# A five-stage transformer kernel: state sums as accumulating transposes, and two of eight input products on TensorE

## The reference

```
xc, z  = split(layernorm(x) @ W_in.T)              # 512 channels each
xc     = silu(causal_conv4(xc) + conv_b)
delta, Bm, Cm = split(xc @ W_x.T)                  # 64 + 16 + 16
delta  = softplus(delta @ W_dt.T + b_dt)
h[t]   = exp(delta[t] * A) * h[t-1] + delta[t] * Bm[t] * xc[t]   # 16 states a channel
y      = sum over the 16 states of h * Cm, plus Dp * xc
x     += (y * silu(z)) @ W_out.T
```

## Time and profile before

| | us |
|---|---|
| median of 3 runs | 2305.53 (2303.75 to 2313.75) |
| the profiled execution's own time | 2302.67 |
| its span | 2300.9 |
| TensorE busy, mean granted clock | 1823.9, 0.899 |
| VectorE busy | 1546.7 |
| ScalarE busy | 1047.7 |
| POOL busy | 1245.8 |
| scan L1074, 128 times | 292.6 |
| POOL's product L1009, 128 times | 301.7 |
| TensorE's sums L822, 512 passes | 246.9 |
| input products L1068, 128 times | 157.7 |

### The profile page before, as it was taken

One profiled execution on the slowest core, in us unless ns is written; L12 is line 12 of the kernel. 1 busy time (PEld: TensorE's weight loads), 2 busy tenths in 40 slices (PEclk: granted clock), 3 DMA queues, 4 the chain that ended last, 5 costly groups with the idle time before them and its releaser, 6 DMA issues. The chain is left out here.

```text
span 2300.9 us, 37782 instructions
## 1 busy us (share of the span) xinstructions
PE 1823.9 (79%) x10904; PEld 1250.3 (54%) x10905; DVE 1546.7 (67%) x3360; ACT 1047.7 (46%) x3013; POOL 1245.8 (54%) x999
## 2 busy tenths in 40 slices
PE   6799968988898668999869999798547999998000
PEld 6478833343433243677538888466414888877000
DVE  7699829999999968333447777577796333335633
ACT  1667637666666323333147777555225333332000
POOL 2688617777777710788415555365002555554775
PEclk9799989999999977999989999899666999999555
DMA  9121012312121052899601111000503999997332
GB/s 292 35 96 54 8 62 120 104 44 91 57 78 70 1 163 76 231 296 249 153 10 34 34 34 29 20 2 2 197 0 110 287 283 290 287 284 226 114 114 87
DMA packets 163772, 271.45 MB, mean 118 GB/s; under 512 B 28690, under 2 KB 97780, under 8 KB 162676
## 3 DMA queue, kind: packets, MB, share of 16 engines
q1 hardware_dynamic: 103028, 173.97, 23.4%
q0 software_dynamic: 30464, 68.19, 11.7%
q10 hardware_dynamic: 30144, 27.62, 3.5%
HBM read 218.17 MB, written 51.53 MB: 117 GB/s over the span
## 5 line engine op out<-in xcount | busy, mean ns | idle before, releaser
L1009 POOL TENSOR_TENSOR b_h<-b_h,b_bcb 128x1024 f32<-128x1024 f32 x128 | 301.7, 2359 | 115.4 <-DVE b_h L1074 115.0
L1583 POOL DMA_INDIRECT m1x_xb<-scratch_xn,m_tok x192 | 182.8, 952 | 316.2 <-issue 196.9
L1074 DVE TENSOR_TENSOR_SCAN b_h<-b_dA,b_pbx 128x1024 f32<-128x1024 f32 x128 | 292.6, 2286 | 4.4
L822 PE MATMUL b_psy<-b_h,ident 128*128 128x512 f32 x512 | 246.9, 611 | 56.0 <-POOL b_h L1009 56.0
L1630 PE MATMUL m1x_psh<-m1x_xe,m1x_w 128*128 128x128 f32 x1536 | 208.5, 279 | 11.2 <-issue 10.8
L1630 PEld LDWEIGHTS m1x_psh<-m1x_xe,m1x_w 128*128 128x128 f32 x1536 | 188.4, 193 | 19.2 <-issue 18.5
L822 PEld LDWEIGHTS b_psy<-b_h,ident 128*128 128x128 f32 x512 | 93.2, 192 | 191.7 <-POOL b_h L1009 104.6
L1772 DVE TENSOR_TENSOR m1x_hT<-m1x_sg,m1x_psh 128x128 f32<-128x128 f32 x192 | 55.3, 288 | 207.4 <-ACT m1x_sg L1718 138.3
L956 ACT ACTIVATE b_dA<-b_delta,b_A 128x504 f32<-128x504 f32 x256 | 166.1, 705 | 52.4 <-DVE b_h L1074 49.9
L1958 POOL TENSOR_TENSOR x_s<-x_s,x_rs 128x1024 f32<-128x1024 f32 x64 | 121.1, 1893 | 126.9 <-DVE x_rs L2124 126.9
L1068 DVE TENSOR_TENSOR b_pbx<-b_pdx,b_bcb 128x1024 f32<-128x1024 f32 x128 | 157.7, 1232 | 20.5 <-ACT b_pdx L939 13.8
(11 more groups left out here) (452 smaller groups left out, 4330.9 us busy)
## 6 DMA issues: line engine op xcount, KB each, us to landing
m1x_w<-in_m_w SPq DMA_DIRECT2D x192, 256.0 KB
b_bcb<-scratch_bc_rows SPq DMA_DIRECT2D x64, 512.0 KB, 4.7
scratch_y<-m1x_yb ACTq DMA_DIRECT2D x192, 128.0 KB
m_w<-in_m_w SPq DMA_DIRECT2D x64, 368.0 KB
a_c<-in_ctxT SPq DMA_DIRECT2D x16, 512.0 KB, 4.7
m_w<-in_m_w SPq DMA_DIRECT2D x64, 128.0 KB
x_area<-in_ctxT SPq DMA_DIRECT2D x32, 256.0 KB
m_w2all<-in_m_w SPq DMA_DIRECT2D x1, 8192.0 KB
```

Of the source, the lines that this page charges most:

```text
L822: mm = pe.matmul(psy[:, k % 2, :], ident[:, :], h[:, u % HB, j, :], start=False, stop=(nq == NQ - 1 and j == CQ - 1))
L1009: q.tensor_tensor(hs, hs, bcb[:, 1, CQ * nq:CQ * nq + CQ], ALU.mult).then_inc(sem("hc"), 1)
L1074: v.tensor_tensor_scan(h[:, u % HB].rearrange("p j n -> p (j n)"), dA[:, u % DB].rearrange("p j n -> p (j n)"), pbx[:, :, :].rearrange("p ...
L1583: g.indirect_dma_start(out=xb[:, j, :], out_offset=None, in_=xn, in_offset=bass.IndirectOffsetOnAxis(ap=tok[:, b:b + 1], axis=0)).then_inc ...
```

## The change

- `stage_mla`: the products of `turn` become accumulating transposes (`is_transpose=True`). On TensorE `output(t - 3)` is called before `queries(t + 1, 0)`, on ScalarE `exps(t - 1)` before `turned(t - 2, 0)`.
- `stage_mamba`, sums: `summed` turns h while it accumulates, 8 transposes of 128 x 128 in place of 2 products of 512 columns, so that `psy` holds tokens x channels. It has one buffer (one bank) now. The gate z is therefore computed by tokens: Z for 384 channels, the new piece W for the last 128. After the gate the new piece Y turns y back to channels (4 transposes and a copy), once a chunk.
- `stage_mamba`, inputs: for the pairs nq = 3 and 7 (TQ) the product dx * B is made on TensorE: dx is turned once a chunk (piece E), B of these pairs is computed by tokens once a group (piece U) and spread to diagonals (piece P, 16 copies of 128 columns on ScalarE), and `turned_inputs` multiplies the two, 8 products of 128 columns, two steps ahead. VectorE keeps six products of eight.
- Buffers: `pbx` two, `pdx` one, h five. B is broadcast for six pairs only.
- The last group's first three output parts stand together before its last `summed`; the last part is turned first.
- `stage_moe`: five products of 512 columns (WARM) at the head of TensorE's stream in the routing part of both expert stages; their result isn't used.

```diff
@@ stage_mla @@
-                                           ident[:, :], start=(j == 0), stop=(j == LOOK - 1))
+                                           ident[:, :], is_transpose=True, start=(j == 0), stop=(j == LOOK - 1))
@@ stage_mamba @@
-    HB, DB = 6, 4
+    HB, DB = 5, 4
+    TQ = (3, 7)
+    VQ = [nq for nq in range(NQ) if nq not in TQ]
-        pdx = ps("pdx", [P, 2, GT])
-        pbx = ps("pbx", [P, CQ, GT])
-        psy = ps("psy", [P, 2, GT])
+        pdx = ps("pdx", [P, GT])
+        pbx = ps("pbx", [P, 2, CQ, GT])
+        psy = ps("psy", [P, NTT, P])
...
         PE_AT = {"Z": (32, 33, 34, 35), "T": (4, 7), "O": (69, 70, 72, 73), "X": (10, 11, 13, 15), "V": (12, 14, 16, 18),
-                 "B": (22,), "D": (25, 28, 29, 30)}
-        ACT_AT = {"N": (6, 6, 9, 9), "T": (9, 12), "X": (15, 16, 18, 20), "V": (17, 19, 21, 23), "S": (24,), "B": (27,),
-                  "D": (30, 33, 34, 35), "L": (30, 36), "Z": (37, 38, 39, 40), "G": (41,), "I": (33, 41, 47, 55)}
-        POOL_AT = {"A": (28, 35, 36, 37), "M": (29, 37, 43, 51)}
+                 "B": (22,), "U": (23,), "W": (35,), "D": (25, 28, 29, 30), "Y": (44, 52, 60, 68), "E": (29, 37, 45, 53)}
+        ACT_AT = {"N": (6, 6, 9, 9), "T": (9, 12), "X": (15, 16, 18, 20), "V": (17, 19, 21, 23), "S": (24,), "B": (27,), "U": (29,),
+                  "D": (30, 33, 34, 35), "L": (30, 36), "Z": (37, 38, 39, 40), "W": (40,), "G": (41,), "Y": (49, 57, 65, 73), "I": (34, 42, 50, 58),
+                  "E": (34, 42, 50, 58), "P": (31, 32, 38, 40)}
+        POOL_AT = {"A": (28, 35, 36, 37), "M": (28, 36, 43, 51)}
...
+                    elif name == "U":
+                        for t in range(NTT):
+                            for c in range(NCH):
+                                mm = pe.matmul(psw[:, s, t * NBT:(t + 1) * NBT]..., xc[:, g % 2, c, t * P:(t + 1) * P], wxt(c), ...)
+                    elif name == "E":
+                        pe.wait_ge(sem("dx"), NCH * g + r + 1)
+                        for t in range(NTT):
+                            mm = pe.transpose(psw[:, s, t * P:(t + 1) * P], dx[:, t * P:(t + 1) * P], ident[:, :])
+                    elif name == "Y":
+                        pe.wait_ge(sem("gated"), NCH * g + r + 1)
+                        for t in range(NTT):
+                            mm = pe.transpose(psw[:, s, t * P:(t + 1) * P], yT[:, t, :], ident[:, :])
                     elif name == "O":
-                        pe.wait_ge(sem("yz"), NCH * (g + 1))
+                        for c in range(NCH):
+                            taken(pe, "Y", g, c)
...
+                def turned_inputs(u):
+                    g, k, q = u // NU, u // NQ, TQ.index(u % NQ)
+                    pe.wait_ge(sem("dxT"), k + 1)
+                    pe.wait_ge(sem("bdiag"), NTQ * CQ * g + CQ * q + CQ)
+                    pe.wait_ge(sem("scan"), u - 1)
+                    for j in range(CQ):
+                        for t in range(NTT):
+                            mm = pe.matmul(pbx[:, u % 2, j, t * P:(t + 1) * P], dxT[:, t, :], bdiag[:, q, j, t, :], start=True, stop=True)
+                    mm.then_inc(sem("tx"), 1)
@@ summed @@
-                    if nq == 0 and k >= 2:
-                        pe.wait_ge(sem("sums_out"), k - 1)
+                    if nq == 0:
+                        if k:
+                            pe.wait_ge(sem("sums_out"), k)
+                        for t in range(NTT):
+                            pe.matmul(psy[:, t, :], xc[:, g % 2, c, t * P:(t + 1) * P], ddiag[:, c, :], start=(t == 0), stop=False)
                     pe.wait_ge(sem("hc"), u + 1)
                     for j in range(CQ):
-                        mm = pe.matmul(psy[:, k % 2, :], ident[:, :], h[:, u % HB, j, :], start=False,
+                        for t in range(NTT):
+                            mm = pe.matmul(psy[:, t, :], h[:, u % HB, j, t * P:(t + 1) * P], ident[:, :], is_transpose=True, start=False,
@@ TensorE's loop over steps @@
+                        if (i + 2) % NQ in TQ:
+                            turned_inputs(NU * g + i + 2)
                         for n, q, r in due(PE_AT, g, i):
                             piece(n, q, r)
+                        if g == NG - 1 and i == NU - 1:
+                            for c in range(NCH - 1):
+                                last_output(c)
                         summed(g, i)
-                        if g == NG - 1 and i % NQ == LAST and i >= NQ:
-                            last_output(i // NQ - 1)
@@ ScalarE @@
                     elif name == "I":
                         k = NCH * g + r
                         a.wait_ge(sem("dx"), k + 1)
-                        if k >= 2:
-                            a.wait_ge(sem("scan"), NQ * (k - 1))
-                        a.activation(pdx[:, k % 2, :], dx[:, :], ACT.Copy).then_inc(sem("pdx"), 1)
+                        if k:
+                            a.wait_ge(sem("bx"), NV * k)
+                        a.activation(pdx[:, :], dx[:, :], ACT.Copy).then_inc(sem("pdx"), 1)
+                    elif name == "P":
+                        q, j = r // CQ, r % CQ
+                        if g:
+                            a.wait_ge(sem("tx"), NTQ * (NCH * g - 1) + q + 1)
+                        for t in range(NTT):
+                            ins = a.activation(bdiag[:, q, j, t, :], ident[:, :], ACT.Copy, scale=BT[:, t, r:r + 1])
+                        ins.then_inc(sem("bdiag"), 1)
@@ scanned, VectorE @@
-                    v.tensor_tensor(pbx[:, :, :], bc(pdx[:, (NCH * g + c) % 2, None, :], [P, CQ, GT]), bcb[:, 0, CQ * nq:CQ * nq + CQ],
-                                    ALU.mult).then_inc(sem("bx"), 1)
+                    if nq in VQ:
+                        if n == 0:
+                            v.wait_ge(sem("pdx"), k + 1)
+                        if u >= 2:
+                            v.wait_ge(sem("scan"), u - 1)
+                        v.tensor_tensor(pbx[:, u % 2], bc(pdx[:, None, :], [P, CQ, GT]), bB[:, n], ALU.mult).then_inc(sem("bx"), 1)
+                        v.wait_ge(sem("bx"), NV * k + n + 1)
+                    else:
+                        v.wait_ge(sem("tx"), NTQ * (NCH * g + c) + TQ.index(nq) + 1)
@@ stage_moe, routing @@
+                    for n in range(WARM):
+                        pe.matmul(psl[:, 0:8, :].rearrange("p t e -> p (t e)"), ident[:, :], X[:, 0:2, :].rearrange("p t d -> p (t d)"), start=True, stop=True)
```

146 lines of the change are left out of this document (97 added, 49 removed).

## The result

The changed kernel takes 2329.09 us (median of 5 runs, 2326.17 to 2330.5) against 2308.31 for the kernel before (5 runs beside it). The ratio is 1.0091, 95% interval 1.0066 to 1.0115: slower by 21 us, outside the range that I gave. (Now and then one execution of a kernel, of that of before too, takes far longer, 2668.31 us once; the ratios leave these out.) The profiled execution took 2329.09 us, and its span is 2327.4, 26.5 more than that of before.

A forecast was written before the change was run, and what follows sets the result against it. TensorE was taken to bound attention, VectorE the state stage, TensorE's small passes at 1.2 GHz the routing. Terms -11 - 12 + 7 + 4 - 4 = -16 on 2302.67 gave 2286.7, as a median 2289 us; range 2250 to 2309.

The forecast's parts named there:

- Attention: Attention loop: a tile falls from 12.91 to 12.18 us and the two last turnings halve; -11 us in all.
- Unit prices: TensorE: 0.112 us per 128-column pass, 0.43 per 512. VectorE: state step 3.48 us with a product, 2.21 without.
- Routing: Expert stages: five products ahead of the routing raise TensorE's clock for a while; -2 us in each of two parts.
- Start and end: State stage: +7 us before the first scan, +4 after the last, from added work and outputs ahead of the last sum.
- The places: Sign of being right: VectorE gaps before the scans at steps 3, 7 and 19 of a group, with TensorE named.
- the chain at the group change: State steps: ScalarE's functions delay the copy of sums, then TensorE's inputs; VectorE stalls 4.9 us at step 3.
- State steps, what comes into the path: State stage: stalls at group changes, outputs and step 19 use up most of the gain, leaving -12 us for all steps.
- TensorE 95 us of 102: State steps: TensorE's listed work in a group is 95 us, uneven, within a group of 102 us.
- rival 2: State steps without convolution or output work: TensorE's clock falls to 1.2 GHz, 37 us over the forecast, near 2320; chance 0.10.
- rival 3: Accumulating transposes need more than one pass: state steps +25 us, no attention gain, 2338 us; chance 0.05.
- rival 1: State steps: overlap is better, shorter group-change stalls and none at step 19; steps -48 us, near 2250; chance 0.28.
- an ideal 58 us: State steps: two of eight products leave VectorE, so 466 us of steps could be 408, before any stalls.

The follow-up runs named there:

- e5: Changed kernel without turned inputs, all eight products of inputs and rows of B on VectorE; ratio to the kernel before 0.9947.
- e2: Changed kernel with ScalarE's copy of a chunk's sums one step earlier, ahead of the softplus functions; ratio to the kernel before 1.0007, state steps 473.7 us.
- e14: e8 with three of four convolution taps left out in groups 1 to 3; ratio to the kernel before 0.9856, state steps 441.5 us.
- e7: Changed kernel with one convolution tap of four in groups 1 to 3; ratio to the kernel before 1.0066, state steps 483.0 us.
- e1: Changed kernel with the sums over states as plain products with the identity, not transposes; ratio to the kernel before 1.0278, state steps 535.4 us.
- e6: Changed kernel with the B columns from four transposes, not 32 products, at step 26 instead of 23; ratio to the kernel before 1.009.
- e9: e8 with sums as plain products in steps 28 to 31 and 0 to 7 of every group and the whole last group; ratio 0.9967.
- e11: Changed kernel without turned inputs, with ScalarE's copies of the sums and of the fourth turned chunk one step earlier; ratio to the kernel before 0.989.
- e13: e11 with last output products split, first copy of inputs one step earlier, group outputs and their additions one to two steps later; ratio 0.9868.
- e8: Changed kernel with the edits of e2 and e6, the fourth turned chunk's copy ahead of the gate functions, turned inputs at steps 5 and 7; ratio 0.9932.
- e10: e8 with the first diagonals of B two steps later, the first copy of inputs one step earlier, last output products split; ratio 0.9889.
- e15: e8 with last output products split, first copy of inputs one step earlier, outputs and their additions one to two steps later; ratio 0.9928.

## Why the prediction was wrong

**What held.** Attention: a tile takes 12.09 us (206.74 to 218.83) where I forecast 12.18, VectorE without a wait. Unit prices: steps of 3.44 and 2.20 us when nothing stalls, VectorE 101.8 us in the second group to the tenth. Routing came to -4.0 against -4, but by luck: I had -2 in each part and it was -0.6 and -3.4, and over all kernels with the five products, e5 aside, the two parts together take 219.7 to 226.1 us, against 227.1 before. Start and end were each 2 us dearer than forecast; in the start the two writings of diagonals P take 1.3 us each for the 0.8 that I had estimated. The places were right as well: the gaps lie before the scans of steps 3 and 19 and the addition at step 7, TensorE is named, and the chain at the group change runs through L and G as described. That of step 3 was right in its times up to TensorE: counted from the end of scan 31 (462.6), L begins at 5.1 (forecast 5), the copy of the sums ends at 12.5 (12.3) and VectorE wants step 3 at 11.4 (11), but TensorE's three pieces then end at 17.7 and not 15.9, for 2.9 of their 5.2 us at the lower clock.

**The step that failed** is "State steps, what comes into the path", the sum of -12 for the steps: +26.8 came. Three terms of it were mis-sized. By groups it gave 105.6, 117.1, 117.1 and 113.3 us, and 118.5, 129.8, 128.7 and 116.0 came. The second group (excess of a step over its plain 3.44 or 2.20):

| steps | forecast | measured |
|---|---|---|
| 3, and 31 with late inputs | 4.9 + 1.4 | 6.4 + 1.7 |
| 7 and 8 (outputs) | 4.7 + 0.5 | 7.5 + 1.9 |
| 19 | 3.8 | 3.7 |
| 27 | 0 | 3.4 |
| 0, 11, 15, 16, 23 | 0 | 4.6 |

1. *TensorE 95 us of 102.* It was 107.7. The items listed add to 96, and the price of a pass was low: by the same prices the second group of before has 101 us of passes, where the trace showed 104.9 at a clock of 1.00, so about 4 of the missing 12 us could have been found beforehand. By line, overlaps counted twice: sums 35.2 for 28.8, turned inputs 18.6 for 14.4, outputs 9.4 for 6.9, the diagonal products 6.4 for 3.6, turnings 5.5 for 3.6. At a clock of 0.99 it is still 102.7 (second group of e2), more than VectorE's 101.8. I had set 95 beside 102 and gone on as if VectorE were the bound with single stalls; in fact TensorE had the more work, neither was full (107.7 and 101.8 of 129.8 us), and each waited for the other at several places. That TensorE's work counts is shown by e14 (9.9 us less work, 6 us less in that group, 13.7 in all), by e7 (9.2 less, 4.3 less) and from the other side by e1 (25.6 us more work, 13 us more in that group). It counts for about half of its size there, so it isn't a bound by itself.
2. *Stalls, each followed alone.* The chain through ScalarE's functions was known, at 4.9. One step's earlier copy took off 19.2 us over three changes, 6.4 each on average, and the turned inputs' place another 10.9. Two waits had no term at all: that of step 27, behind the B columns (3.4 us; gone in e6), and in the first group, forecast 105.6 and measured 118.5, one for ScalarE's copy of dx at step 8, behind the gate functions:

```profile
374.88 1.23 DVE L1162 TENSOR_TENSOR b_pbx<-b_pdx,b_bB 128x1024 f32<-128x1024 f32 x1 [3.24 <-ACT b_pdx L1001]
```

3. *The clock at its upper level throughout.* I had put it at nothing in the forecast and left it to rival 2. It was 0.91, 0.91, 0.93 and 0.84 in the four groups, 101 us of the 493 at the lower level. Where TensorE was already late this cost about 5 us a group (e2's two groups), some 15 us of the 39 that the forecast missed; this last figure is an estimate from one pair of groups and not separately shown.

**The rivals.** Rival 2 named 2320 for the clock, and it is in part what came: the clock did fall in many windows. But its condition, more than half of the quiet chunks at 1.2 GHz, wasn't met (the lowest chunk of the sixteen has a mean clock of 0.74), and its place was another: the clock fell after TensorE's waits at the group changes and made the stalls there longer. That 2320 is 9 us from what came is luck, and rival 3's 2338 is as near. A clock of 1.00 in the last group by plain products was slower (e9), as was a higher clock throughout (e1), and the lowest clock went with one of the shortest stages (e11). So in these runs the clock cost where TensorE was what VectorE waited for. The Trainium skill, "TensorE: Matmul & The Clock Gate", Part 4: PE-mode transpose, says that a transpose doesn't count as PE-busy the same way and the full clock doesn't engage for it. The trace agrees in direction: with the sums of the last group as transposes the clock was 0.84 to 0.87, as plain products 0.96 and 1.00 (e1, e9). The plain products are also more work. In the last chunk of the last group the kernel before, busy 17.4 of 27.4 us with plain products, was at 1.00 and the changed one, busy 16.6 of 24.8, at 0.79, but the width of the passes differs there. And stretches that hold transposes among other products ran at 1.00 (502.0 to 556.6). Rival 3 (no single pass) is refuted: a step's sums are 8 records and 1.04 us. Rival 1's 2250 was the opposite of what came; the best steps here, 453.7 us, are 12 us under those of before, where rival 1 had 48.

**What the change was worth by part** (shown by ratios): attention and routing 0.9914; the change without the turned inputs 0.9947, with ScalarE's two copies in the right order 0.989, with the mends of e13 0.9868, the best of all kernels here that compute the whole (2215.28 against 2244.16 us). The turned inputs cost 1.4% in the order given. In the best orders that I found they gain nothing: the steps are equal (455.2 against 453.8), and with the later start the whole is 0.4% slower (0.9932 against 0.989, e8 and e11) or 0.2% with the ends mended, which is not clear of the noise (0.9889 against 0.9868, e10 and e13). Not tried: the copy of dx ahead of the gate functions, turned inputs for one step of eight only, and a second bank for the sums, which would have to come from `pbx`, since all eight are in use (`pbx` four, `psw` two, `pdx` and `psy` one each).

## What to carry to other kernels

Before work is moved from a full engine to another, add up the receiver's whole load with the new work at both clock levels and put it beside the giver's new load: here, at 102 against 102, the move paid nothing out of an ideal 58 us. Check the prices first by adding up the old kernel with them. Where a single bank and an in-order queue link two engines, look first for what stands ahead of the copy that frees the bank; one position in ScalarE's order was worth 19 us here. And look at every copy that stands behind the same functions: mending one wait uncovered the next (e13, e15). The lower clock followed waits here as well as transposes; it cost where the waiting engine was the late one, and filling it with work to lift the clock made things worse (e9).

## What the runs showed of the hardware that I had not expected

- fp32 transposes that accumulate over 64 calls into one bank take one record each: 258 records in the window of a group (256 are its own) and 35.2 us; as plain products with the identity 512 records and 66.1 us (e1).
- Less work on TensorE went with a lower clock that gave most of it back: in e6 a wait of 2.18 us was followed by turned inputs of 3.62 us instead of 1.95, and in e7 the step behind the shortened work ran at a clock of 0.5.
- A mended stall uncovered another: with the outputs one to two steps later the 6.5 to 7.0 us at step 7 became 3.4, and step 8, at most 4.0 before, took 5.1 to 7.0, now for ScalarE's copy of dx; the state steps are 453.8 and 453.7 (e11, e13).
